# Sums of squares in four column groups and the query norm as the exponential's scale, in a two-layer local-attention kernel

## The reference, cut to what matters

```python
# branch B, one layer; x is (batch, 1024, 128), 8 heads of 64
h = shift_token(x)                       # second half of the features from the token before
q, k, v = split(h @ wqkv)                # to heads
q = q / clip(norm(q), 1e-12) * q_scale   # norm over the 64 numbers of a head
k = k / clip(norm(k), 1e-12) * k_scale
q, k = rotary_xpos(q, k)                 # q*cos*scale + rotate_half(q)*sin*scale, k the same with 1/scale
sim = (8*q) @ k.T                        # window of 64 queries against 128 keys, band mask
x = x + (softmax(sim) @ v) @ wo
h = layernorm(shift_token(x)) ; a, g = split(h @ w1 + b1) ; x = x + (a * gelu(g)) @ w2 + b2
```

## Time and profile before

| | |
|---|---|
| median of 3 runs | 1525.91 us (1513.89 to 1534.49) |
| the profiled execution: its own time | 1533.81 us |
| its span, first to last instruction | 1532.2 us |
| mean granted TensorE clock in it | 0.850 |
| busy: PE, DVE, ACT, POOL | 1272.1, 875.4, 722.5, 283.6 us |

### The profile page before, as it was taken

One profiled execution on the slowest core, in us unless ns is written; L12 is line 12 of the kernel. 1 busy time (PEld: TensorE's weight loads), 2 busy tenths in 40 slices (PEclk: granted clock), 3 DMA queues, 4 the chain that ended last, 5 costly groups with the idle time before them and its releaser, 6 DMA issues. The chain is left out here.

```text
span 1532.2 us, 23584 instructions
## 1 busy us (share of the span) xinstructions
PE 1272.1 (83%) x8754; PEld 687.4 (45%) x8754; DVE 875.4 (57%) x1738; ACT 722.5 (47%) x1912; POOL 283.6 (19%) x219
## 2 busy tenths in 40 slices
PE   5799699888679879978859988897886998889787
PEld 4682163254368235225438624521634852442263
DVE  5426755964442776586453386567544438646754
ACT  1326275466232647447422355743842335664283
POOL 1003220510100421241010051133201014103220
PEclk9659799989855989998975698998997569899799
DMA  6003200310100310130010031013001013102200
GB/s 252 1 1 100 62 2 27 111 26 14 30 1 1 122 41 2 52 106 6 14 30 1 21 108 34 1 56 106 3 14 30 1 39 99 26 1 85 77 16 14
DMA packets 39201, 66.38 MB, mean 43 GB/s; under 512 B 5280, under 2 KB 19232, under 8 KB 37152
## 3 DMA queue, kind: packets, MB, share of 16 engines
q1 hardware_dynamic: 37920, 62.43, 13.3%
q10 hardware_dynamic: 1152, 2.26, 0.4%
HBM read 13.29 MB, written 2.10 MB: 10 GB/s over the span
## 5 line engine op out<-in xcount | busy, mean ns | idle before, releaser
L477 POOL TENSOR_TENSOR qk<-pc,ps_ 128x512 f32<-128x512 f32 x128 | 194.1, 1516 | 689.2 <-DVE ps_ L1003 689.2
L837 ACT ACTIVATE prob<-bank,negb 128x128 f32<-128x128 f32 x512 | 185.9, 492 | 73.4 <-DVE negb L1047 73.4
L1003 DVE TENSOR_TENSOR ps_<-rot,tab_s 128x512 f32<-128x512 f32 x128 | 167.6, 1310 | 53.4 <-DMA rot<-raw 52.7
L939 ACT ACTIVATE raw<-bank,vec_s 128x512 f32<-128x512 f32 x128 | 88.0, 688 | 175.6 <-PE bank L493 154.1
L837 ACT ACTIVATION_READ_ACCUMULATOR prob<-bank,negb 128x1 f32 x512 | 150.5, 334 | 0.0
L493 PE MATMUL bank<-hTz,wb_s 128*128 128x512 f32 x256 | 150.1, 681 | 0.4 <-DVE qk L1146 0.4
L712 PE MATMUL bank<-sq,sum_s 128*16 128x512 f32 x256 | 139.5, 628 | 8.2 <-ACT sq L943 8.2
L483 POOL TENSOR_TENSOR prob<-prob,recb 128x512 f32<-128x512 f32 x64 | 66.5, 1039 | 296.4 <-DVE recb L1068 296.4
L544 PEld LDWEIGHTS bank<-vbd,a_probT 128*128 128x128 f32 x512 | 116.6, 334 | 0.0
L1047 DVE TENSOR_REDUCE negb<-bank 128x8 f32<-128x1024 f32 x64 | 78.3, 1224 | 66.8 <-PE bank L602 66.5
L544 PE MATMUL bank<-vbd,a_probT 128*128 128x18 f32 x512 | 110.8, 363 | 0.0
(11 more groups left out here) (144 smaller groups left out, 2140.3 us busy)
## 6 DMA issues: line engine op xcount, KB each, us to landing
rot<-raw SPq DMA_DIRECT2D x256, 128.0 KB, 2.0
vS<-vB SPq DMA_DIRECT2D x24, 512.0 KB, 4.6
vS<-vB SPq DMA_DIRECT2D x8, 384.0 KB, 5.7
xn_tok<-x SPq DMA_DIRECT2D x5, 512.0 KB, 3.6
tab_s<-tabs SPq DMA_DIRECT2D x1, 2048.0 KB, 21.6
vS<-x SPq DMA_DIRECT2D x4, 512.0 KB, 3.8
out<-vS SPq DMA_DIRECT2D x8, 256.0 KB, 2.4
wb_s<-wb SPq DMA_DIRECT2D x1, 1536.0 KB, 17.2
```

The costliest lines, as they stand in the source:

```text
L477: pool.tensor_tensor(dst, pc[:, j % 2, :], ps_[:, j % 2, :], ALU.add).then_inc(sum_rdy, 1)
L837: ins = act.activation(prob[:, t % 2, g, h, :], s_bank[t % 2][:, g, h * P:(h + 1) * P], ACT.Exp, bias=negb[:, t % 2, g, h:h + 1], accum_ou ...
L939: act.activation(raw[:, jb % 4, :], bank[:, i % RING, :], ACT.Identity, scale=vec_s[:, g:g + 1]).then_inc(raw_rdy, 1)
L1003: dve.tensor_tensor(ps_[:, j % 2, :], rot[:, jb % 4, :], st, ALU.mult).then_inc(prod_rdy, 1)
```

## The change

Only the query and key stage and its uses are touched.

- Keys come first: `qk_tile(k) = (k + 4) % 8` maps the place in the order to the tile, so places 0 to 3 are keys and 4 to 7 queries.
- `sum_squares` runs twice per chunk (after the product of place 5 and after the first value product) with four matmuls each, one for each place of a half, whose outputs go to partitions 0, 32, 64 and 96 of one bank (four column groups); the selection matrix is 128x32. `sq` has four slots, ACT's square of place k waits for the group sum that read its slot.
- The sums are copied as 128 partitions and turned by four 128x128 transposes instead of 16x128 ones. `norms` writes 1/norm into a buffer of its own, `inv_norm`, and splits only the keys' part (32 columns instead of 64).
- Only the key tiles are spread and multiplied: 4 products and 4 DVE operations per chunk instead of 8. In chunk 1 one `scale` stands before each `rotate` instead of two; the ring has 12 uses instead of 16 there, and 4 instead of 8 after it.
- The query's 1/norm is used in the window stage: as `scale` operand from memory of each of the 512 exponentials, and DVE multiplies the negated maxima by it in one more small operation (linked behind the reduce).

```diff
 def qk_use(l, c, k):
-    return USE0[f"qk{l}{c}"] + (k if c == 0 or k < 4 else 4 + 3 * (k - 4))
+    return USE0[f"qk{l}{c}"] + (k if c == 0 or k < 4 else 4 + 2 * (k - 4))
+def qk_tile(k):
+    return (k + 4) % B_QK
 def norm_use(l, c, k):
-    return USE0[f"norm{l}"] + k if c else USE0[f"qk{l}1"] + 4 + 3 * (k // 2) + 1 + k % 2
+    return USE0[f"norm{l}"] + k if c else USE0[f"qk{l}1"] + 4 + 2 * k + 1
...
+        inv_norm = sb("inv_norm", [P, CHUNKS, TPC, 4, 4])
-        sq = sb("sq", [P, 2, CH])
+        sq = sb("sq", [P, 4, CH])
-        ss = sb("ss", [16, 2, CH])
+        ss = sb("ss", [P, 2, CH])
...
+        def query_norm(t):
+            return inv_norm[:, t // TPC, t % TPC, :, 2:4]
...
-                        def sum_squares(c, k):
-                            j = pair(l, c, k)
-                            taken(pe, qk_use(l, c, k))
-                            pe.matmul(bank[0:16, 4 + c, :], sum_s[:, k, :], sq[:, j % 2, :], start=(k == 0),
-                                      stop=(k == B_QK - 1)).then_inc(ss_done, 1)
+                        def sum_squares(c, part):
+                            for m in range(4):
+                                k = 4 * part + m
+                                taken(pe, qk_use(l, c, k))
+                                mm = pe.matmul(bank[32 * m:32 * m + 32, 4 + c, :], sum_s[:, part, :], sq[:, m, :],
+                                               start=(part == 0), stop=(part == 1), skip_group_check=True)
+                            mm.then_inc(ss_done, 1)
                         def turn_sums(c):
                             pe.wait_ge(sums_copied, l * CHUNKS + c + 1)
                             for tt in range(TPC):
-                                mm = pe.transpose(bank[:, 4 + c, tt * 16:(tt + 1) * 16],
-                                                  ss[0:16, c, tt * P:(tt + 1) * P], ident_s[0:16, 0:16])
+                                mm = pe.transpose(bank[:, 4 + c, tt * P:(tt + 1) * P],
+                                                  ss[:, c, tt * P:(tt + 1) * P], ident_s[:, :])
...
-                                if k:
-                                    sum_squares(c, k - 1)
+                                if k == 5:
+                                    sum_squares(c, 0)
                                 if c and k == 3:
                                     turn_norms(0)
                                 if c and k >= 4:
-                                    spread_norms(0, (2 * k - 8, 2 * k - 7))
+                                    spread_norms(0, (k - 4,))
...
                                 if tt == 0:
-                                    sum_squares(c, B_QK - 1)
+                                    sum_squares(c, 1)
...
-                        spread_norms(1, range(B_QK))
+                        spread_norms(1, range(4))
...
                                 ins = act.activation(prob[:, t % 2, g, h, :], s_bank[t % 2][:, g, h * P:(h + 1) * P],
                                                      ACT.Exp, bias=negb[:, t % 2, g, h:h + 1],
+                                                     scale=query_norm(t)[:, h, g:g + 1],
                                                      accum_out=sumb[:, t % 2, g, h:h + 1])
...
-                                if jb >= 2:
-                                    act.wait_ge(ss_done, jb - 1)
-                                act.activation(sq[:, j % 2, :], bank[:, i % RING, :], ACT.Square)\
+                                if jb >= 4:
+                                    act.wait_ge(ss_done, jb // 4)
+                                act.activation(sq[:, jb % 4, :], bank[:, i % RING, :], ACT.Square)\
                                    .then_inc(drained[i % RING], 1)
...
-                        dve.tensor_reduce(negb[:, t % 2, :, :], s_bank[t % 2].rearrange("p g (h k) -> p g h k", h=4),
-                                          AX_X, ALU.max, negate=True).then_inc(win_max, 1)
+                        b_ = negb[:, t % 2, :, :]
+                        link(dve.tensor_reduce(b_, s_bank[t % 2].rearrange("p g (h k) -> p g h k", h=4),
+                                               AX_X, ALU.max, negate=True))
+                        dve.tensor_tensor(b_, b_, query_norm(t).rearrange("p h g -> p g h"), ALU.mult).then_inc(win_max, 1)
...
                                 if c and k >= 4:
-                                    scale(0, (2 * k - 8, 2 * k - 7))
-                                r = 0 if k < 4 else 2
+                                    scale(0, (k - 4,))
+                                r = 2 if k < 4 else 0
                                 rotate(l, c, k, qk_use(l, c, k), tab_s[:, r, cc(c)], tab_s[:, r + 1, cc(c)])
...
-                        scale(1, range(B_QK))
+                        for k in range(4, B_QK):
+                            dve.wait_ge(sum_rdy, pair(l, 1, k) + 1)
+                        scale(1, range(4))
```

More of the change, by code:

```diff
@@ L168, in program @@
         pm = vS[:, TILES - 2:TILES, :]
-        with nc.sbuf_tensor("rT", [48, 2, CH], BF16) as rT:
+        with nc.sbuf_tensor("rT", [24, 2, CH], BF16) as rT:
             pass
-        ss = sb("ss", [16, 2, CH])
+        ss = sb("ss", [P, 2, CH])
         vbd = sb("vbd", [P, T // (2 * A_WIN), A_KV, 2 * A_E])
@@ L177, in program @@
         nw = sb("nw", [P, 4, 64])
-        rsp = sb("rsp", [P, 2, TPC, 48], BF16)
+        rsp = sb("rsp", [P, 2, TPC, 24], BF16)
         a_max = sb("a_max", [P, 4, A_W])
@@ L275, in linker, with inv_root @@
             return link
-        def inv_root(dve, link, src, c, op, n):
+        def inv_root(dve, link, src, c, op, n, root=None):
             v, y, t, s = (nw[:, r, 0:n] for r in range(4))
+            if root is not None:
+                v, t, s = (z.rearrange("p (a e) -> p a e", e=4) for z in (v, t, s))
+                y = root
             link(dve.tensor_scalar(v, src, c, None, op))
@@ L927, in copy_norms @@
                             act.wait_ge(rt_full, l * CHUNKS + c + 1)
-                            act.activation(rT[:, c, :], bank[0:48, 6 + c, 0:256].bitcast(BF16), ACT.Copy)\
+                            act.activation(rT[:, c, :], bank[0:24, 6 + c, 0:256].bitcast(BF16), ACT.Copy)\
                                .then_inc(rt_rdy, 1)
@@ L951, in _ @@
                                 if tt == 0:
-                                    act.wait_ge(ss_done, (l * CHUNKS + c + 1) * B_QK)
-                                    act.activation(ss[:, c, :], bank[0:16, 4 + c, :], ACT.Copy)\
+                                    act.wait_ge(ss_done, (l * CHUNKS + c + 1) * 2)
+                                    act.activation(ss[:, c, :], bank[:, 4 + c, :], ACT.Copy)\
                                        .then_inc(sums_copied, 1)
@@ L1130, in norms @@
                             dve.wait_ge(sums_turned, l * CHUNKS + c + 1)
-                            inv_root(dve, link, bank[:, 4 + c, 0:64], 1e-24, ALU.max, 64)
-                            y, r_ = nw[:, 1, :], nw[:, 2, :]
-                            part = [rsp[:, c, :, 16 * m:16 * (m + 1)] for m in range(3)]
-                            y, r_ = (z.rearrange("p (t k) -> p t k", t=TPC) for z in (y, r_))
+                            y = inv_norm[:, c, :, :, :].rearrange("p t k e -> p (t k) e")
+                            inv_root(dve, link, bank[:, 4 + c, :].rearrange("p (t e) -> p t e", e=32)[:, :, 0:4], 1e-24,
+                                     ALU.max, 64, y)
+                            y = inv_norm[:, c, :, :, 0:2]
+                            r_ = nw[:, 2, 0:32].rearrange("p (t k e) -> p t k e", t=TPC, k=4)
+                            part = [rsp[:, c, :, 8 * m:8 * (m + 1)].rearrange("p t (k e) -> p t k e", k=4) for m in range(3)]
                             link(dve.tensor_copy(part[0], y))
@@ L1145, in scale @@
                                 dve.wait_ge(mm_full, i + 1)
-                                dve.tensor_tensor(qk[:, k, cc(c)], bank[:, i % RING, :], qk[:, k, cc(c)], ALU.mult)\
+                                z = qk[:, qk_tile(k), cc(c)]
+                                dve.tensor_tensor(z, bank[:, i % RING, :], z, ALU.mult)\
                                    .then_inc(drained[i % RING], 1)
@@ L1262, in host_constants @@
     ones = np.full((P, P), 1.0 / P, f)
-    sum_heads = np.zeros((P, B_QK, 16), f)
-    for k in range(B_QK):
-        sum_heads[:64, k, 2 * k] = 1
-        sum_heads[64:, k, 2 * k + 1] = 1
+    sum_heads = np.zeros((P, 2, 32), f)
+    for part in range(2):
+        sum_heads[:64, part, 2 * part] = 1
+        sum_heads[64:, part, 2 * part + 1] = 1
     r = np.arange(P)
@@ L1280, in host_constants @@
     parts += [np.tile(window, (1, 4)), np.tile(first, (1, 4))]
-    seln = np.zeros((P, B_QK, P), f)
-    for k in range(B_QK):
+    seln = np.zeros((P, 4, P), f)
+    for k in range(4):
         for m in range(3):
-            seln[16 * m + 2 * k, k, :64] = 1
-            seln[16 * m + 2 * k + 1, k, 64:] = 1
```

(2 more changed lines are left out.)

20 lines of the change are left out of this document (10 added, 10 removed).

## The result

The change makes the kernel slower. Its median is 1551.24 us (1546.95 to 1554.95, 4 runs), against 1526.12 us for the kernel before in the same comparison (1513.89 to 1534.49, 4 runs): a ratio of 1.017, 95% interval 1.0096 to 1.0244. The profiled execution took 1554.95 us, 21.1 more than that of before, and its span 1553.3; its mean granted clock is 0.808 against 0.850.

The account below looks back on a forecast made before the run. DVE and POOL were taken to pace the query and key stages, ACT the window stages. Gains of 48.8 us against losses of 38.4 and 2 made -8.4 on 1533.81; scaled to the median, 1517 us, range 1477 to 1552.

Parts of the forecast that it names:

- The scale operand: Window-stage exponentials: a second operand from memory adds 97 ns, seven of eight tiles exposed; 4.8 us per stage, 38.4 in all.
- rival A: Window-stage exponentials: the scale operand costs nothing, being fetched with the bias; 1479 us, faster by 3%; chance 14%.
- The step that failed first: End of the window stage: ACT's work stretched, PE's left at its old speed; no term put down.
- Rival C: Query and key stage: PE pauses lower its clock, losing chunk 0's gain and delaying chunk 1's end; 1549 us; chance 13%.
- the earlier start of chunk 1 in layer 0: Query and key stage: vS DMAs and row swaps come earlier, by 1.9 us in layer 0, 2.3 in layer 1.
- The rounds: Chunk 1's four rounds: the dropped multiplication gains nothing, 2.48 us against 2.50; waits for PE go, 1.2 us per stage.
- rival D: Chunk 1's rounds: DVE and POOL don't block each other; 1.9 us instead of 2.48, total 1499 us; chance 10%.
- Norms and multiplications of chunk 1: End of chunk 1, per stage: turned sums in time 0.9 us, four multiplications fewer 2.4, 0.5 taken back for half clock.
- The group of four: PE's squares in the query and key stage: four matmuls run nearly at once, 1.3 us; bounds 0.96 and 3.84.
- rival B: Query and key stage: a group's matmuls run one after the other, 3.84 us; +32 us, 1557 us; chance 8%.
- The maxima: Window stage: one more small DVE operation delays ACT only at the first tile; 0.25 us per stage, 2 in all.
- the milder form of rival B: Query and key stage: a group of four takes 2.4 us; total about 1530 us; no separate chance given.

Follow-up runs that it names:

- experiment 1: Changed kernel without the exponentials' scale operand, the queries' normalisation left out, the small operation on the maxima kept: 1485.2 us, ratio 0.9784.
- experiment 2: Kernel before, with each of the 512 exponentials taking its scale from a column of ones in memory: 1596.17 us, ratio 1.0486.
- experiment 5: Changed kernel with the exponentials keeping the scale operand but losing the bias, the maxima still made: 1485.86 us, 2.6% under the median of before.
- Experiment 4: Changed kernel with two unread PE products near the end of each window stage, before tile 6's values are weighed: 1536.67 us, ratio 1.0121.
- experiment 6: Kernel before with the groups of squares and turned sums alone, queries first, both spread, no scale operand: 1521.97 us, ratio 0.998.
- Experiment 3: Changed kernel with three unread PE products before the sums of chunk 0 are turned, in layer 0: 1537.84 us, ratio 1.0123.
- experiment 8: Changed kernel with both fillings, chunk 0 of layer 0 and the end of each window stage: 1523.67 us, ratio 0.9962.
- experiment 10: Changed kernel without the bias operand, with unread PE products in chunk 0 of layer 0 and two pauses of chunk 1: 1475.56 us, ratio 0.9614.
- experiment 9: Kernel before with the groups alone and unread PE products in chunk 0 of layer 0 and two pauses of chunk 1: 1501.65 us, ratio 0.9815.
- experiment 7: Kernel before with the groups alone and three unread PE products before chunk 0's sums are turned in layer 0: 1501.04 us, ratio 0.9846.

## Why the prediction was wrong, by its own steps

The forecast was 1517 us and the measurement is 1551.24, just inside the range (to 1552). It is within the 2% that had 0.72, but the interval of the ratio lies wholly above 1: slower, where slightly faster was forecast. The sum was -8.4 us on the profiled execution, and it is +21.1. Term by term:

- **The scale operand, foreseen 38.4 us, measured 42.** Price (97 ns, measured 93), place and exposure hold: 5.1 and 5.4 us per stage instead of 4.8, 42 in all. Experiments 1, 2 and 5 show that it is this, from three sides. Taking the nearest row for a second operand was right, though no row had decided it, and rival A is out.
- **The step that failed first: nothing was put down for the end of the window stage.** The prediction stretched ACT's work and left PE's at its old speed. A longer ACT means a thinner PE; its clock fell, and 1.5 to 1.8 us per stage and the output products came on top, 13 + 2.5 us. Experiment 4 gave them back with two idle products per stage. Rival C had this mechanism, but only for the query and key stage.
- **The second: the earlier start of chunk 1 in layer 0, foreseen 1.9, measured 0.1.** This is rival C in the place that it named, and with the sign that it named: the pause before the turned sums was 3.42 us, and the clock fell to 0.50. "Against: the pauses are shorter than that one" was no argument, since this pause, though shorter than the one of the earlier trace rows, had its effect. Nor is the effect the same each time: behind the same 3.42 us the last value copy ends at 22.9 us in all four passes of the changed kernel, and at 22.9, 22.3, 21.7 and 21.7 in those of experiment 6. Experiment 3 shows the gain that was there: 3.5 us per pass, more than foreseen. In layer 1 the clock held and the term was 2.8 instead of 2.3. C's other place, the end of chunk 1, cost nothing that shows: in layer 0 the clock is 0.50 there from 1304 to 1312, and the eight rounds take 17.50 us in both layers.
- **The rounds: right in their pace, and in the sum by an average.** Nothing came from the multiplication that went, since POOL's addition took its place: 2.50 us as worked out, and rival D is out. The waits for PE gave 1.2 and 1.3 us (foreseen 1.2), but the prediction read them as an even 1.15 per stage, and they aren't: the last four rounds of the kernel before take 13.0 us in two of the eight stages and 10.5 to 11.1 in the others, against 10.0 after the change. In one of the two (stretch 162 to 170 us) PE works at clock 0.50 behind a pause of 4.80. The Trainium skill (SBUF — State Buffer, SBUF: two separate sides) has an operation of VectorE with two SBUF inputs and one of GpSimd that reads SBUF on an exclusive lock, which blocks the second for the whole instruction of the first. `pc` with 1.36 us agrees: POOL's addition starts ahead of it and ends at 1309.07, and `pc` ends 0.54 later.
- **Norms and multiplications of chunk 1, foreseen 2.8 (0.9 + 2.4 - 0.5), measured 2.25 in both layers.** The four multiplications take 2.48 us as foreseen and the wait for the turned sums is gone, but the norms now begin as POOL's last addition does, and their second operation waits for its end; in the kernel before it was over by then. A wait that goes moves what stood behind it; what it then meets was not looked at.
- **The group of four, foreseen 1.3:** 1.28 us at full clock, 1.94 at half (experiment 6). Three times as fast as one after the other (3.84); rival B is out. The Trainium skill (TensorE: Matmul & The Clock Gate, Measured speedup vs the span model) has 2.38 times for three column tiles of 32 and 3.07 for four row tiles; 3.0 for four column groups in fp32 lies with these.

```profile
1272.49 1.28 PE L726 MATMUL bank<-sq,sum_s 128*32 128x512 f32 x8
```

- **The maxima, foreseen 0.25 us per stage:** from the reduce to the first exponential 1.46 us instead of 1.26.

For the query and key stages this makes -38.3 where -46.8 stood (with the maxima), for the window stages +55.2 where +38.4 stood, and +4 outside. Of the 29.5 us between, PE's clock took 15.7 at the end of the window stages and 7.1 at the start of chunk 1 in layer 0, the norms 4.4, the operand itself 3.6 and the stretches between passes 0.8; the start of chunk 1 in layer 1, the rounds and the maxima gave back some 2. The mechanism that carried the forecast was right; what turned the sign is PE's clock, in two places. With both filled (experiment 8) the ratio is 0.9962, about the 0.5% less that the forecast had. Rival C had a chance of 0.13 and was weighed for one stage only. That its figure, 1549, lies 2 us from the measurement is luck: it has 4 us in each of eight query and key stages, and there its mechanism took 1.8 in four.

Two slips in the working change nothing here: the ratio written as 0.9945 is 0.9948 (1525.91 of 1533.81), from which 1517.5 does follow, and the milder form of rival B comes to some 1526 us by its own numbers, not 1530.

## What to carry to other kernels

Price an operand by what it adds to each instruction times the instructions, on the engine that paces the stage: a [128, 1] scale on 512 exponentials of 128 columns costs more than the 64 multiplications of 128x512 that it replaces, and costs nothing once it takes the bias's place. Time taken from TensorE is no gain where another engine paces, and turns into a loss where it opens a pause before work on the path; look at the granted clock in the stretch after each pause that a change opens, in every stage whose pace changes, not only in those that it edits. Idle products of known length in such a pause gave back 13 and 15 us in the changed kernel, nothing in two pauses of experiment 10, and nothing in experiment 9, where they ran late.

## What the runs showed of the hardware that was not expected

Times of the same kernel differ by up to 2% (the kernel before beside experiments 5 to 8: 1503.36 to 1534.32 us, but for one run of 2270.53, whose cause is unknown), and the differences come in steps. From the end of a pass's last window stage to the first `raw` copy of the next the profiled executions have some 134 us or some 141 (once 135.5), and before the first pass 114.4 or some 121, with the same code. It is branch A's attention, outside the change. Those of the kernel before and of the changed one have the long form in all four places, so the 21 us between them hold none of it; that of experiment 5 has the short form in three, those of experiments 1, 7, 8 and 9 in two. Stretch 82 to 89 us of experiment 7 and of the kernel before (columns as above):

```profile
82.00:89.00 7.00, 6.88 (x106) 6.75 (x103) 4.95 (x9) 2.49 (x5) 0.00 (x0) 0.97 0.01 2
```

```profile
82.00:89.00 7.00, 7.00 (x71) 6.88 (x67) 2.67 (x4) 1.30 (x3) 0.00 (x0) 0.50 0.01 2
```

PE is busy all the time in both, with small transposes and scores, and gets through 106 instructions at clock 0.97 and through 71 at 0.50. In some passes the clock rises in this stage and the pass is 7 us shorter; in most it stays down. A busy PE alone doesn't bring the clock up, then; what decides it was not tried, nor whether an edit elsewhere changes how often it happens. It gives each run a lottery of up to four such steps, which is the likely reason that the kernel before had medians of 1513.74, 1526.25 and 1530.47.
